# The state scan of a Mamba layer: eight of sixteen states go through TensorE, and GpSimd multiplies two

## The chip, the cores and the metric

One NeuronCore of one Trainium2 chip runs the whole program. The metric is the device time of one execution in microseconds (us). Kernels are told from each other by the median of several executions; a difference within 0.5% is taken as no difference.

The engines are TensorE (PE, with its weight loads shown apart as PEld), VectorE (DVE), ScalarE (ACT), GpSimd (POOL) and SyncE (SP, which only starts DMAs here). Each runs its own list of instructions in order, and they meet at semaphores.

## What is computed

The model is a chain of four blocks over x of 4 sequences x 1024 tokens x 256 channels: attention with a linear bias, two layers of windowed attention with a feed-forward part, a selective state scan (Mamba), and a mixture of 32 experts. The change touches only the core of the third:

```python
A = -jnp.exp(A_log)
def step(h, inputs):
    dt_t, x_t, B_t, C_t = inputs
    h = jnp.exp(dt_t[..., None] * A) * h + (dt_t * x_t)[..., None] * B_t[:, None, :]
    y = jnp.einsum('bds,bs->bd', h, C_t)
    return (h, y)
...
y = jnp.swapaxes(ys, 0, 1) + x * D
y = y * silu(z)
```

There are 512 inner channels d and 16 states s. For each sequence, channel and state a recurrence of first order runs over 1024 tokens; its result is multiplied by C (one row of 1024 values per sequence and state, the same for all channels) and summed over the 16 states.

## The kernel before

The program is nine phases one after the other. The scan is `phase_scan` (L2201), whose tiles have names beginning with H in the profile. It runs between the phase that makes its inputs and the mixture of experts.

**Tiling.** A tile is 128 channels of one sequence over all 1024 tokens: 4 sequences x 4 tiles = 16 tiles g. In each tile 16 states s are done one after the other, so there are 256 units n = (g, s). The text names a unit by its state within its tile: unit 2 is the third of a tile, and unit 16 is the first of the next.

**What every unit does.** ACT makes `decay` = exp(ndt x rate) in one of two PSUM buffers (L2367). POOL makes `feed` = ndu x B in one of four buffers (L2396, AHEAD = 4). DVE runs the recurrence (L2449).

**The product with C has three forms**, chosen by the letter of the state in `CLASS` (L2207):

- D: DVE itself multiplies by a row of C that was broadcast to 128 partitions (`times_c`, L2425), into `part`.
- P: the scan writes `handed`, and POOL multiplies (`shared_product`, L2406), into `pool_part`.
- T: the scan writes `turning`; PE transposes its eight 128x128 blocks (`turn`, L2490) into the PSUM tile `p_T`; ACT copies them back to SBUF, each scaled per partition by C (`weigh`, L2352), into `sT`; PE multiplies them with the negative identity, which turns them back and adds them (`bring`, L2500).

In the forms D and P, PE adds the part with four matmuls of the profile (`add`, L2508). All sums gather in one PSUM tile `p_y`, which starts with the term x * D (`skip_term`, L2469). DVE ends a tile with `tail` (L2433), which reads `p_y`; it is issued after unit 1 of the next tile.

**Orders that are written by hand.** They decide what waits behind what:

- ACT, for each n: decay(n), which waits until unit n-2 has been scanned (and, if it is D, multiplied); then weigh(n-2) if that unit is T.
- POOL, for each n: feed(n), which waits until unit n-4 has been scanned; then the product of unit n-2 if that is P.
- DVE, for each n: scan(n), times_c(n) if D, and after unit 1 the tail of the tile before.
- PE, for each n: add of the P unit n-4, bring of the T unit n-2, add of the D unit n-1, turn(n) if T. `skip_term` of a tile stands ahead of its first bring or add, and waits for the tail of the tile before, because `p_y` is single.
- SP loads the rows of B for each sequence, and rows of C broadcast for the states that are D or P (`weighted`).

Of the kernel before, what the change touches and what calls it, by code (L numbers as in the profile page):

```python
# [15 lines left out]
P = 128  # L16
# [2184 lines left out]
def phase_scan(nc, T):  # L2201
    with ExitStack() as ctx:
# [1 line left out]
        tiles = [(i, m) for i in range(SEQS) for m in range(XT)]  # L2204
        units = [(g, s) for g in range(len(tiles)) for s in range(NS)]
        NU = len(units)
        CLASS = "TTDPTDTDPTDTPDTD"  # L2207
        NB = SEQ // P
        HB = NB // 2
        NEXT_C = CLASS.index("P", NS // 2)  # L2210
        kind = [CLASS[s] for g, s in units]
        before = {c: list(accumulate((k == c for k in kind), initial=0)) for c in "TDP"}
        per = {c: CLASS.count(c) for c in "TDP"}
        weighted = [s for s in range(NS) if CLASS[s] != "T"]
        row_bytes = [16 if CLASS[s] == "T" else 32 for s in range(NS)]
        AHEAD = 4
# [18 lines left out]
        pool_part = a.sb("pool_part", [P, 2, SEQ])  # L2235
# [14 lines left out]
        p_summed = a.sem("p_summed")  # L2250
# [8 lines left out]
        def reached(eng, sem, value):  # L2259
            if value > 0:  # L2260
                eng.wait_ge(sem, value)

        def use_of(n):

            i = units[n][0] // XT
            return before["T"][n] + 1 + i + (n % (XT * NS) > (XT - 1) * NS + NEXT_C and i + 1 < SEQS)

        def use_of_c(i):
            return before["T"][(XT * i - 1) * NS + NEXT_C] + i if i else 0
# [111 lines left out]
        @block.gpsimd  # L2381
        def _(pool):
            pool.wait_ge(fixed, 48)
            for m in range(XT):
                nc.gpsimd.tensor_scalar(skip_diag[:, m, :], ident[:, :], skip[:, m:m + 1], None, ALU.mult)
            nc.gpsimd.tensor_scalar(minus[:, :], ident[:, :], -1.0, None, ALU.mult).then_inc(diag_ready, 1)

            def feeds(n):
                g, s = units[n]
                i, m = tiles[g]  # L2390
                if s == 0:
                    pool.wait_ge(dt_loaded[g % 2], 32 * (g // 2 + 1))
                if m == 0:
                    pool.wait_ge(row_loaded[s], row_bytes[s] * (i + 1))
                reached(pool, scanned, n - AHEAD + 1)
                nc.gpsimd.tensor_tensor(feed[:, n % AHEAD, :], ndu[:, g % 2, :], bs[:, s, :], ALU.mult  # L2396
                                        ).then_inc(fed, 1)

            def shared_product(n):
                g, s = units[n]  # L2400
                k = before["P"][n]
                if tiles[g][1] == 0:
                    pool.wait_ge(row_loaded[s], 32 * (tiles[g][0] + 1))
                pool.wait_ge(scanned, n + 1)
                reached(pool, p_summed, k - 1)
                nc.gpsimd.tensor_tensor(pool_part[:, k % 2, :], handed[:, k % 2, :], cs[:, weighted.index(s), :], ALU.mult  # L2406
                                        ).then_inc(pool_parted, 1)

            for n in range(NU + 2):
                if n < NU:  # L2410
                    feeds(n)
                if n >= 2 and kind[n - 2] == "P":
                    shared_product(n - 2)

        @block.vector
        def _(dve):
# [40 lines left out]
        @block.tensor  # L2457
        def _(pe):
            started = set()

            def skip_term(g):

                if g in started:
                    return
                started.add(g)
                reached(pe, yg_ready, g)
                pe.wait_ge(tail_loaded[g % 2], 32 * (g // 2 + 1))
                for c in range(2):
                    nc.tensor.matmul(p_y[:, c, :], skip_diag[:, tiles[g][1], :],  # L2469
                                     xs[:, g % 2, c * CHUNK:(c + 1) * CHUNK], start=True, stop=False)  # L2470

            def turn_c(i):
                u = use_of_c(i)
                pe.wait_ge(c_loaded, 16 * (i + 1))
                for h in range(2):
                    if u:
                        pe.wait_ge(copied, 2 * u + h - 1)
                    for b in range(HB):
                        at = (h * HB + b) * P
                        last = nc.tensor.transpose(p_T[:, h, b, 0:NS], c_rows[:, at:at + P], ident[0:NS, 0:NS])  # L2480
                    last.then_inc(turned, 1)

            def turn(n):
                u, k = use_of(n), before["T"][n]
                pe.wait_ge(scanned, n + 1)
                for h in range(2):
                    pe.wait_ge(copied, 2 * u + h - 1)
                    for b in range(HB):
                        at = (h * HB + b) * P
                        last = nc.tensor.transpose(p_T[:, h, b, :], turning[:, k % 3, at:at + P], ident[:, :])  # L2490
                    last.then_inc(turned, 1)

            def bring(n):
                g, s = units[n]
                skip_term(g)
                k = before["T"][n]
                for h in range(2):
                    pe.wait_ge(copied, 2 * use_of(n) + h + 1)
                    for b in range(HB):
                        last = nc.tensor.matmul(p_y[:, h, b * P:(b + 1) * P], sT[:, k % 2, h * HB + b, :], minus[:, :],  # L2500
                                                start=False, stop=False)
                last.then_inc(t_summed, 1)

            def add(n, src, done):
                g, s = units[n]
                skip_term(g)
                for c in range(2):
                    last = nc.tensor.matmul(p_y[:, c, :], minus[:, :], src[:, c * CHUNK:(c + 1) * CHUNK],  # L2508
                                            start=False, stop=s == NS - 1)
                last.then_inc(done, 1)  # L2510

            pe.wait_ge(fixed, 48)
            pe.wait_ge(diag_ready, 1)
            turn_c(0)
            for n in range(NU + 5):
                if 0 <= n - 4 < NU and kind[n - 4] == "P":
                    k = before["P"][n - 4]
                    pe.wait_ge(pool_parted, k + 1)
                    add(n - 4, pool_part[:, k % 2, :], p_summed)
                if 0 <= n - 2 < NU and kind[n - 2] == "T":  # L2520
                    bring(n - 2)
                if 0 <= n - 1 < NU and kind[n - 1] == "D":
                    k = before["D"][n - 1]
                    pe.wait_ge(parted, k + 1)
                    add(n - 1, part[:, k % 3, :], d_summed)
                if n < NU:
                    i = units[n][0] // XT + 1
                    if units[n] == (XT * i - 1, NEXT_C) and i < SEQS:
                        turn_c(i)
                    if kind[n] == "T":  # L2530
                        turn(n)
# [517 lines left out]
def build(nc, T):  # L3049
    with nc.allow_non_contiguous_dma(reason="weights' columns, biases and slots, a few elements each"):  # L3050
        phase_qkv(nc, T)
        phase_attention(nc, T)
        for layer in range(2):
            phase_window(nc, T, layer)
            phase_feed_forward(nc, T, layer, layer == 1)
        phase_front(nc, T)
        phase_scan(nc, T)
        phase_moe(nc, T)
# [21 lines left out]
```

## Time and profile before

| | us |
|---|---|
| median of 3 executions | 3718.92 (3718.04 to 3734.68) |
| the profiled execution | 3717.85 |
| its span in the profile | 3716.1 |
| around the span | 1.75 |
| the scan phase, from its first ACT decay to the end of its last tail | 2670.8 to 3405.4 |
| mean granted TensorE clock | 0.949 |

| engine, whole program | busy us | share |
|---|---|---|
| PE | 3243.4 | 87% |
| DVE | 2436.9 | 66% |
| ACT | 1875.8 | 50% |
| POOL | 1444.3 | 39% |

The phases follow each other without overlap, so these shares say little about a change in one of them. The scan takes about a fifth of the time and has its own limits; the stretch between two tails is one tile. In the timeline, pieces are named by tile, line and count, a number in brackets is the idle time of that engine before the piece, and the name behind it is what ended that idle time. Where PE's pieces overlap by some tenths of a us, that is the pipelining of matmuls: the distance from one start to the next is what counts.

### The profile page before, as it was taken

What the parts mean: (1) busy time and instruction counts of PE and PEld (TensorE: products, weight loads), DVE (VectorE), ACT (ScalarE), POOL (GpSimd) and SP (SyncE); (2) the same over time, 40 slices, a digit from 0 to 9 for tenths busy, and PEclk for the clock granted to TensorE, in tenths of its full rate; (3) what the DMA queues carried; (4) which work ended last, traced back from release to release, by engine and by line L of the source; (5) the groups of instructions that cost most, each with busy time, mean ns of one, the idle gap of its engine ahead of it and who ended that gap; (6) DMA issues with size and microseconds to landing.
All of it is one profiled execution on the core that took longest, in us unless ns stands there. A gap on an engine that the chain in (4) does not pass through costs nothing. (4 is left out here: it accounts for less than half of the span.)

```text
span 3716.1 us, 52305 instructions
## 1 busy us (share of the span) xinstructions
PE 3243.4 (87%) x18096; PEld 1976.8 (53%) x18096; DVE 2436.9 (66%) x4589; ACT 1875.8 (50%) x4007; POOL 1444.3 (39%) x993
## 2 busy tenths in 40 slices
PE   8599999879999799799999799799288888887898
PEld 4244444346666555466666455333156565555766
DVE  8488888456666522266666332389499999996633
ACT  2177777646666411166666311165377777774100
POOL 4101111122222211122222111134599999996523
PEclk9699999989999899899999899899599999999899
DMA  5956565120000141200000321233535151512874
GB/s 169 150 65 95 84 84 79 33 68 22 22 22 22 52 164 54 67 19 22 22 22 20 90 72 48 77 132 144 193 133 199 57 199 57 199 57 80 297 220 124
DMA packets 275715, 347.29 MB, mean 93 GB/s; under 512 B 70976, under 2 KB 206640, under 8 KB 274812
## 3 DMA queue, kind: packets, MB, share of 16 engines
q1 hardware_dynamic: 259596, 305.70, 30.1%
q10 hardware_dynamic: 10736, 25.94, 2.0%
q0 software_dynamic: 5120, 12.30, 0.9%
q8 instruction: 145, 2.38, 0.3%
q14 instruction: 118, 0.97, 0.1%
HBM read 227.72 MB, written 112.80 MB: 92 GB/s over the span
## 5 line engine op out<-in xcount | busy, mean ns | idle before, releaser
L2396 POOL TENSOR_TENSOR H_feed<-H_ndu,H_bs 128x1024 f32<-128x1024 f32 x256 | 595.2, 2364 | 5.8 <-DMA H_cs<-between_bc 3.1
L852 ACT ACTIVATE B_probs<-B_p_exp,B_key_bias 128x512 f32<-128x512 f32 (+3 forms) x768 | 394.8, 583 | 144.0 <-PE B_p_exp L910 113.4
L750 DVE TENSOR_REDUCE B_part_max<-B_p_max 128x1 f32<-128x512 f32 (+3 forms) x768 | 374.6, 545 | 84.0 <-PE B_p_max L874 81.5
L1283 ACT ACTIVATE D_probs<-D_scores,D_neg,D_rq 128x256 f32<-128x256 f32 x512 | 283.1, 573 | 289.1 <-DVE D_neg L1198 289.1
L2367 ACT ACTIVATE H_decay<-H_ndt,H_rate 128x1024 f32<-128x1024 f32 x256 | 287.8, 1125 | 196.3 <-DVE H_turning L2449 103.1
L1137 POOL TENSOR_TENSOR D_rnorm<-D_norm,D_power 128x8 f32<-128x8 f32 x64 | 106.2, 1659 | 506.6 <-DVE D_norm L1153 506.6
L871 PE MATMUL B_p_max<-B_k,B_q 100*128 100x512 bf16 (+3 forms) x768 | 256.9, 341 | 43.2 <-DMA B_key_bias<-in_key_bias 33.2
L1700 PE MATMUL E_p_ag<-E_hT,E_w 128*128 128x512 f32 x640 | 283.2, 602 | 2.1 <-ACT E_hT L1656 2.1
L2449 DVE TENSOR_TENSOR_SCAN H_turning<-H_decay,H_feed 128x1024 f32<-128x1024 f32 x112 | 253.5, 2274 | 23.2 <-POOL H_feed L2396 22.2
L2500 PEld LDWEIGHTS H_p_y<-H_minus,H_sT 128*128 128x128 f32 x1792 | 224.9, 200 | 76.2 <-ACT H_sT L2352 56.2
L2500 PE MATMUL H_p_y<-H_minus,H_sT 128*128 128x128 f32 x1792 | 233.4, 287 | 35.6 <-ACT H_sT L2352 35.6
L907 PE MATMUL B_p_exp<-B_q,B_k 100*128 100x512 bf16 (+3 forms) x768 | 250.3, 330 | 11.4 <-ACT B_probs L852 6.5
L1672 ACT ACTIVATE E_gated<-E_p_ag,E_b 128x512 f32<-128x512 f32 x96 | 62.6, 652 | 373.9 <-PE E_p_ag L1700 354.7
L2352 ACT ACTIVATE H_sT<-H_p_T,H_cT 128x128 f32<-128x128 f32 x896 | 242.9, 388 | 12.7 <-PE H_p_T L2490 12.3
L1345 PE MATMUL D_p_qk<-D_wqkv,D_hT 128*128 128x512 f32 x512 | 242.0, 616 | 1.1 <-ACT D_hT L1258 1.1
L1195 DVE CUSTOM_DVE_ANT_0 D_scores<-D_scores,D_mask 128x256 f32<-128x256 f32 x512 | 202.1, 457 | 55.6 <-PE D_scores L1372 55.3
L2449 DVE TENSOR_TENSOR_SCAN H_decay<-H_decay,H_feed 128x1024 f32<-128x1024 f32 x96 | 218.9, 2280 | 15.7 <-POOL H_feed L2396 15.5
L1700 PEld LDWEIGHTS E_p_ag<-E_hT,E_w 128*128 128x128 f32 x640 | 122.0, 193 | 155.5 <-issue 154.5
L1141 POOL TENSOR_TENSOR D_rnorm<-D_norm,D_power 128x8 f32<-128x8 f32 x64 | 129.9, 2029 | 188.3 <-DVE D_norm L1153 188.3
L1627 DVE SCALAR_TENSOR_TENSOR E_act_out<-E_p_ag,E_b,E_gated 128x512 f32<-128x512 f32 x96 | 67.7, 706 | 197.3 <-ACT E_gated L1672 197.3
L871 PEld LDWEIGHTS B_p_max<-B_k,B_q 100*128 100x128 bf16 x768 | 75.2, 98 | 221.4 <-DVE B_part_max L750 132.0
L2508 PE MATMUL H_p_y<-H_part,H_minus 128*128 128x512 f32 x384 | 185.0, 604 | 8.4 <-DVE H_part L2425 8.4
(259 smaller groups left out, 6874.9 us busy)
## 6 DMA issues: line engine op xcount, KB each, us to landing
H_bs<-between_bc SPq DMA_DIRECT2D x64, 512.0 KB, 7.5
H_cs<-between_bc SPq DMA_DIRECT2D x36, 512.0 KB, 8.2
B_q<-between_q_parts SPq DMA_DIRECT2D x96, 128.0 KB
B_k<-between_k_parts SPq DMA_DIRECT2D x96, 128.0 KB
between_slots_x<-E_clear ACTq DMA_DIRECT2D x4, 2570.0 KB, 22.0
I_xe<-between_slots_x ACTq DMA_DIRECT2D x32, 257.0 KB, 4.0
D_base<-between_z SPq DMA_DIRECT2D x64, 128.0 KB, 2.2
between_z<-D_z SPq DMA_DIRECT2D x64, 128.0 KB, 1.7
```

Source lines behind the costliest of these rows:

```text
L750: nc.vector.reduce_max(part_max[:, g % 2, kc, qb, h:h + 1], p_max[:, use % 3, 0:keys], AX.X).then_inc(maxed, 1)
L852: nc.scalar.activation(probs[:, x % PROBS, skip:512], p_exp[:, n % SCORES, skip:512], ACT.Exp, bias=key_bias[:, g % SETS, kb - 4 * Q + 4, ...
L871: last = nc.tensor.matmul(p_max[:, use % 3, 0:keys], q[0:KR, u, h, qb * P:(qb + 1) * P], k[0:KR, u, h, 512 * kc:512 * kc + keys], start=Tr ...
L907: last = nc.tensor.matmul(p_exp[:, n % SCORES, skip:512], k[0:KR, u, h, kb * P:(kb + 1) * P], q[0:KR, u, h, 512 * Q + skip:512 * Q + 512], ...
L1283: last = nc.scalar.activation(probs[:, place[m], :, :].rearrange("p a b -> p (a b)"), scores[:, place[m], :, :].rearrange("p a b -> p (a b ...
L1345: last = nc.tensor.matmul(p_qk[:, m, :], hT[:, i % 2, k, :], wqkv[:, k, m * INNER:(m + 1) * INNER], start=k == 0, stop=k == KD - 1)
L1700: last = nc.tensor.matmul(p_ag[:, m % 2, n, :], w1[:, k, at:at + P], hT[:, i % 2, k, :], **flags)
L2352: last = nc.scalar.activation(sT[:, k % 2, h * HB + b, :], p_T[:, h, b, :], ACT.Copy, scale=cT[:, i % 2, h * HB + b, s:s + 1])
L2367: nc.scalar.activation(decay[:, n % 2, :], ndt[:, g % 2, :], ACT.Exp, scale=rate[:, m, s:s + 1]).then_inc(decayed, 1)
L2396: nc.gpsimd.tensor_tensor(feed[:, n % AHEAD, :], ndu[:, g % 2, :], bs[:, s, :], ALU.mult).then_inc(fed, 1)
L2449: nc.vector.tensor_tensor_scan(out, decay[:, n % 2, :], feed[:, n % AHEAD, :], 0.0, ALU.mult, ALU.add).then_inc(scanned, 1)
L2500: last = nc.tensor.matmul(p_y[:, h, b * P:(b + 1) * P], sT[:, k % 2, h * HB + b, :], minus[:, :], start=False, stop=False)
```

## The change

`CLASS` becomes a strict alternation. There are now eight T (0, 2, 4, ... 14), six D (1, 3, 7, 9, 13, 15) and two P (5 and 11), where there were seven T, six D and three P (3, 8, 12). POOL makes the product of unit n-4 behind feed(n), and no more that of unit n-2. PE adds a P unit five iterations later, and no more four. The names that are worked out from `CLASS` follow: `weighted` has eight states for nine, so eight rows of C are broadcast, and `NEXT_C`, the state at which C of the next sequence is turned, is 11 for 8.

```diff
-        CLASS = "TTDPTDTDPTDTPDTD"
+        CLASS = "TDTDTPTDTDTPTDTD"
...
-            for n in range(NU + 2):
+            for n in range(NU + AHEAD):
                 if n < NU:
                     feeds(n)
-                if n >= 2 and kind[n - 2] == "P":
-                    shared_product(n - 2)
+                if n >= AHEAD and kind[n - AHEAD] == "P":
+                    shared_product(n - AHEAD)
...
-            for n in range(NU + 5):
-                if 0 <= n - 4 < NU and kind[n - 4] == "P":
-                    k = before["P"][n - 4]
+            for n in range(NU + 6):
+                if 0 <= n - 5 < NU and kind[n - 5] == "P":
+                    k = before["P"][n - 5]
                     pe.wait_ge(pool_parted, k + 1)
-                    add(n - 4, pool_part[:, k % 2, :], p_summed)
+                    add(n - 5, pool_part[:, k % 2, :], p_summed)
```

## Rows read from the trace of the kernel before

**Rows 1.** Busy time of each engine in one tile, by stretch; clock 1.00 is full

```profile
core 0: us, PE busy (x) PEld busy (x) DVE busy (x) ACT busy (x) POOL busy (x), PEclk, DMA share, GB/s
2911.00:2956.00 45.00, 38.21 (x209) 25.77 (x208) 43.47 (x24) 32.18 (x73) 43.82 (x20) 1.00 0.16 59
```

**Rows 2.** Groups of the scan phase: busy us, mean ns, idle before and releasers

```profile
L2396 POOL TENSOR_TENSOR H_feed<-H_ndu,H_bs 128x1024 f32<-128x1024 f32 x256 | 595.2, 2364 | 5.8 <-DMA H_cs<-between_bc 3.1 <-DMA H_bs<-between_bc 2.7
...
L2406 POOL TENSOR_TENSOR H_pool_part<-H_handed,H_cs 128x1024 f32<-128x1024 f32 x48 | 113.1, 2357 | 17.3 <-DVE H_handed L2449 17.3
```

**Rows 3.** Waits of the scan phase: total us, times, longest us

```profile
DVE H_decay L2449 <- POOL H_feed L2396: 15.5, 16, 2.6
ACT H_sT L2352 <- PE H_p_T L2490: 12.3, 8, 2.5
```

**Rows 4.** Timeline, DVE, from one tail to the next: start, us, piece

```profile
2909.30 1.20 DVE L2433 TENSOR_TENSOR H_sz<-H_p_y,H_sz 128x1024 f32<-128x1024 f32 x1
2910.42 2.29 DVE L2449 TENSOR_TENSOR_SCAN H_decay<-H_decay,H_feed 128x1024 f32<-128x1024 f32 x1
2912.81 1.23 DVE L2425 TENSOR_TENSOR H_part<-H_decay,H_cs 128x1024 f32<-128x1024 f32 x1
2913.95 2.28 DVE L2449 TENSOR_TENSOR_SCAN H_handed<-H_decay,H_feed 128x1024 f32<-128x1024 f32 x1
2916.15 2.27 DVE L2449 TENSOR_TENSOR_SCAN H_turning<-H_decay,H_feed 128x1024 f32<-128x1024 f32 x1
...
2946.54 2.30 DVE L2449 TENSOR_TENSOR_SCAN H_decay<-H_decay,H_feed 128x1024 f32<-128x1024 f32 x1 [0.91 <-POOL H_feed L2396]
...
2954.47 1.20 DVE L2433 TENSOR_TENSOR H_sz<-H_p_y,H_sz 128x1024 f32<-128x1024 f32 x1
```

**Rows 5.** Timeline, PE and ACT in the same tile

```profile
2911.00 1.88 PE L2469 MATMUL H_p_y<-H_xs,H_skip_diag 128*128 128x512 f32 x4
...
2918.45 1.12 ACT L2367 ACTIVATE H_decay<-H_ndt,H_rate 128x1024 f32<-128x1024 f32 x1 [1.07 <-DVE H_turning L2449]
2918.47 1.09 PE L2490 MATMUL H_p_T<-H_ident,H_turning 128*128 128x128 f32 x8 [0.30 <-DVE H_turning L2449]
2919.50 2.16 ACT L2352 ACTIVATE H_sT<-H_p_T,H_cT 128x128 f32<-128x128 f32 x8
2920.68 2.19 PE L2500 MATMUL H_p_y<-H_minus,H_sT 128*128 128x128 f32 x16 [1.12 <-ACT H_sT L2352]
2922.71 1.88 PE L2508 MATMUL H_p_y<-H_part,H_minus 128*128 128x512 f32 x4
2924.43 1.04 PE L2490 MATMUL H_p_T<-H_ident,H_turning 128*128 128x128 f32 x8
2925.30 1.88 PE L2508 MATMUL H_p_y<-H_pool_part,H_minus 128*128 128x512 f32 x4
2927.02 1.95 PE L2500 MATMUL H_p_y<-H_minus,H_sT 128*128 128x128 f32 x16
2928.80 1.88 PE L2508 MATMUL H_p_y<-H_part,H_minus 128*128 128x512 f32 x4
```

**Rows 6.** Timeline of the first tile, where DVE waits for ACT

```profile
2714.26 1.04 PE L2490 MATMUL H_p_T<-H_ident,H_turning 128*128 128x128 f32 x8
2714.98 2.18 ACT L2352 ACTIVATE H_sT<-H_p_T,H_cT 128x128 f32<-128x128 f32 x8 [2.52 <-PE H_p_T L2490]
2716.99 2.21 ACT L2367 ACTIVATE H_decay<-H_ndt,H_rate 128x1024 f32<-128x1024 f32 x2
2718.20 2.29 DVE L2449 TENSOR_TENSOR_SCAN H_turning<-H_decay,H_feed 128x1024 f32<-128x1024 f32 x1 [0.89 <-ACT H_decay L2367]
```

**Rows 7.** Timeline, PE, where a bring runs at a lower clock

```profile
2796.47 1.09 PE L2490 MATMUL H_p_T<-H_ident,H_turning 128*128 128x128 f32 x8 [1.39 <-DVE H_turning L2449]
...
2798.68 3.41 PE L2500 MATMUL H_p_y<-H_minus,H_sT 128*128 128x128 f32 x16 [1.12 <-ACT H_sT L2352]
```

**Rows 8.** Timeline, DVE, unit 7 of the first tile

```profile
2697.46 2.30 DVE L2449 TENSOR_TENSOR_SCAN H_decay<-H_decay,H_feed 128x1024 f32<-128x1024 f32 x1
```

## The prediction

> **What bounds the kernel now.** The phases run one after the other, so I read only the scan. The busy time of one tile comes first: in 45.0 us DVE works 43.47 and POOL 43.82, PE 38.21, ACT 32.18 [rows 1]. Two engines are nearly full, and the other two have room. The waits then say which of the two ends last: a D scan waits for a feed 16 times, 15.5 us in all [rows 3], and the timeline puts this once into every tile, ahead of unit 15 (0.91 us) [rows 4]. From tail to tail a tile takes 45.17 us (2909.30 to 2954.47) [rows 4]. So POOL is the bound, but only just. How far below it lies DVE? A D unit takes 3.53 us from scan to next scan (2910.42 to 2913.95), any other 2.19 (2913.95 to 2916.15 shows 2.20, later ones 2.18), the tail 1.12 [rows 4]. With 3.52 for D: 6 x 3.52 + 10 x 2.19 + 1.12 = 44.14 us. That is DVE's floor, and the change leaves it alone: still six D and ten others. **The whole prize is 1.03 us a tile, 15 us in all, 0.4%.**
>
> **Part 1, POOL.** It issues 18 operations a tile for 19, each 2.31 us from start to start (43.82 busy of 45.0, so 44.0 in 45.17, by 19 [rows 1]; 2.36 each in [rows 2], as they overlap a little): 41.7 us for 44.0. Its wait for `handed` (17.3 us in all [rows 2]) goes too: feed(n) and the product of unit n-4 wait for the same scan. POOL is then over 2 us a tile quicker than DVE and keeps up to four feeds in hand; the wait ahead of unit 15 goes: 0.9 us a tile. Nothing waits for the later product: PE wants it five iterations on, some 13 us after the scan, and it comes 5 us after. On SP the loads of the next sequence's rows 5 and 11 wait for it, and all rows queued behind them, some 2.5 us longer; they are needed 12 units later. Nothing. One broadcast row of 25 a sequence goes, from a queue that ends no wait after the start: nothing.
>
> **Part 2, PE and ACT, by their sums.** One add (1.72 us from start to start, 2922.71 to 2924.43) becomes a turn (0.87) and a bring (1.78 to 2.03) [rows 5]. PE: +1.1 us on 38.2. ACT: a weigh more, +2.0 to 2.2 on 32.2. Both stay below 44. By sums alone the change gains.
>
> **Part 3, the order around the tail.** Here I leave the sums and follow the queues, with these steps, all between starts [rows 5, 6]: turn to weigh 0.72 (2714.26 to 2714.98); weigh to its bring 1.18 where PE waits for it; weigh to the next decay 2.01; decay to weigh 1.06; decay to its scan 1.21 (2716.99 to 2718.20); bring to next 2.03 behind a running weigh, else 1.78; add or skip_term 1.72; turn to next 0.87.
>
> Time 0 is a tail's start. Before, units 0 and 1 are both T. Turn(1) is out of the way by the end of the tail, skip_term starts at 1.70 (2911.00), and the next turn is that of unit 4, at 9.17 (2918.47) [rows 4, 5]: between lie units 2 and 3, and that time just holds skip_term, two brings and an add (7.5 us).
>
> After, unit 1 is D and unit 2 is T. PE's order is skip_term, bring(0), add(1), turn(2), and skip_term waits for the tail. It starts at about 1.29 (tail 1.20, then a signal), bring(0) 3.01, add(1) 4.79, turn(2) **6.51**. Unit 2 starts its scan at 1.12 and is ready to be turned at 3.45. Turn(2) is 3.06 us late. On ACT, weigh(2) follows at 7.23, and behind it in the same queue stands decay(5): 9.24. So scan 5 starts at 10.45. DVE could have started it at 9.02 (1.12 + 2.19 + 3.52 + 2.19). **Stall 1.43 us.**
>
> It goes on: bring(2) 8.41, add(3) 10.44, turn(4) 12.16, weigh(4) 12.88, decay(7) 14.89, scan 7 16.10, which DVE could have begun at 14.83 (10.45 + 2 x 2.19). **Stall 1.27 us.** Then bring(4) 14.06, and as unit 5 is P there is no add: turn(6) 16.09, weigh(6) 17.03, bring(6) 18.21, add(7) 20.24, turn(8) 21.96; scan 8 has just ended. PE has caught up. Around the second P (turn(10) behind the added P, at 28.06; weigh 28.78; decay(13) 30.79; scan 13 32.00 for 31.90) another 0.10. Unit 17 starts at 43.42 and the next tail at 46.94.
>
> A tile so takes 44.14 + 1.43 + 1.27 + 0.10 = **46.94 us for 45.17: +1.77**. The same reckoning of the order of before gives 44.14 and POOL's wait, as measured, and that this chain exists is in the trace: in the first tile a turn was late (ACT idle 2.52 us), its weigh held up decay, and DVE stood still for 0.89 us [rows 6].
>
> **Part 4, ends.** Fourteen whole intervals between tails: 24.8 us. Last tile, from its tail on: its unit 15 would start 37.71 us after that tail for 37.24 before (2946.54 less 2909.30): +0.45. First tile: feed arrivals are the same in number of rows; POOL's product no longer stands between feeds, about 2 us better; the late turns of a cold PE cost 1.7 and 1.2 as above; I come to unit 7 at 2698.4 for 2697.46 [rows 8], and as unit 1 is now D the first tail comes another 1.3 later. No row shows this start, so bounds: from -1 to +4; I take +2.0. Sum so far 27.3 us.
>
> **Part 5, TensorE's clock.** In six tiles of 16 a bring behind a quiet stretch (idle 1.39, a turn, idle 1.12: 3.6 us from one product to the next) ran partly at 1.2 GHz, 3.41 us for 2.19 [rows 5, 7]; the add behind it was slow too, and PE about 1.5 us late. ACT waited for turns 8 times, 12.3 us: once 2.52 [rows 6], once at the very end, and six times about 1.3 behind such a bring; DVE never noticed these six, as there was slack [rows 3]. The order after has a new quiet stretch: from the end of add(15) at 44.4 to skip_term at 48.2, 3.9 us with only a turn in it. Behind it stand exactly skip_term, bring(0), add(1), turn(2), where every us is a stall of DVE. If it happens as often as before: 6 x 1.5 = 9 us. Its bounds are none and all 15: 0 to 22.5. Sum **36.3 us**. Against the profiled execution's 3717.85 that is 3754.1; the median lies 1.1 higher, so 3755.
>
> The Trainium skill, TensorE: Matmul & The Clock Gate, section HAM oscillation, says that idle stretches between bursts of matmuls send the clock back to half each time round a loop; its section on PE-mode transpose adds that a transpose does not keep it up. By that the fall would come behind every tail, which is the rival of 3768 below. The trace agrees with it in six of 16 tiles only.
>
> **Rivals.**
> - **The prize is won** (faster side): PE's lateness behind the tail does not reach decay, DVE runs at its floor. 15 x -1.03 = -15.5: 3703. For it: the sums of part 2, and that DVE has three `turning` and three `part` buffers. Against it: ACT's order puts decay(5) behind weigh(2) with no other way round [rows 6]. It decides if turn(2) comes 1.43 us earlier than 6.51, at 5.08.
> - **Half of it**: the first stall comes, but PE makes up the rest before unit 7 (bring(2) starts sooner behind weigh(2), or adds overlap more). 44.14 + 1.43 = 45.57: +0.40 x 15 = 6 us, with the start's +1: 3726.
> - **Half clock behind every tail**: 27.3 + 22.5 = 49.8: 3768. For it: the quiet stretch of 3.9 us in each tile. Against: stretches of 3.6 us did it in six tiles of 16.
> - **The change does not do what it says**: POOL still ends last, because the products bunch. 18 operations are 41.7 us; I give it almost nothing. A PE that stays behind for the whole tile (49 us a tile) would be 3780.
>
> **How the numbers follow.** Forecast 3755, by itself 3742 to 3764 (no low clock with a good start, to ten falls): 0.56. Half clock behind every tail, 0.15. Half of it, 0.13. The prize, 0.13. PE behind all through, 0.03. The measurement of this kernel tells about 0.5% from no change, 18.6 us, which is more than the whole prize: faster by more has 0.03, slower (over 3737.5) the first, second and last, 0.74, and within it the rest, 0.23. The range leaves out the prize and the far tail: 3719 to 3777.
>
> **What would show it.** Right: tail to tail near 47 us; DVE waits for decay ahead of units 5 and 7 of each tile, about 1.4 and 1.3 us, and no more for feeds; POOL's idle time is 5 us a tile; turn(2) starts 6.5 us after the tail's start; some skip_terms and brings behind the tail at half clock. Wrong: tails 44.2 us apart with no wait of DVE, or its waits at other units; turn(2) before bring(0); a wait for `pool_part`.

## The result and the profile after

| | before | after |
|---|---|---|
| median | 3723.2 us | 3774.01 us (3768.62 to 3778.5, 4 executions) |
| ratio | 1 | 1.0139, 95% interval 1.0115 to 1.0163 |
| profiled execution | 3717.85 us | 3770.14 us |
| mean granted clock | 0.949 | 0.946 |

The change costs 1.4%, about 51 us. The forecast was 3755 with a range of 3719 to 3777.

The profiled executions are 52.3 us apart. In the one of after, the first scan starts 4.4 us later, at 2680.13 for 2675.70. The phases ahead of it are untouched, and in the kernels below, which do not touch them either, it starts anywhere between 2670.2 and 2697.7. So what is measured inside the scan is more reliable than the difference of two whole executions. From the first scan to the end of the last tail the scan phase grew by 46.9 us, and the phase behind it by 1.0. Of the first kernel below with turn(2) ahead, two of five executions were disturbed, at 8665.77 and 10821.92 us, and its median and ratio are those of the other three.

First the waits of the scan phase of after (the view of rows 3: total us, times, longest us).

```profile
ACT H_sT L2352 <- PE H_p_T L2490: 93.6, 42, 5.7
...
PE H_p_y L2469 <- DVE H_sz L2433: 44.2, 15, 3.2
DVE H_handed L2449 <- ACT H_decay L2367: 39.0, 15, 4.4
...
DVE H_decay L2449 <- ACT H_decay L2367: 19.0, 17, 1.2
```

Before, DVE waited for a feed once in each tile [rows 3]. Now POOL waits for DVE, and DVE waits for ACT's `decay`: 15 times ahead of a P unit, 39.0 us, and 17 times ahead of a D unit, 19.0 us. ACT in turn waits for PE's transposes, 93.6 us for 12.3 [rows 3], and PE's `skip_term` (L2469) waits for the tail 15 times. That is the chain of the prediction, from its end to its start.

The timeline of one tile shows the steps. It answers to rows 4 and 5; start, us, piece, and in brackets the idle time before it.

```profile
2778.73 1.22 DVE L2433 TENSOR_TENSOR H_sz<-H_p_y,H_sz 128x1024 f32<-128x1024 f32 x1
...
2779.86 2.28 DVE L2449 TENSOR_TENSOR_SCAN H_turning<-H_decay,H_feed 128x1024 f32<-128x1024 f32 x1
...
2780.00 1.98 PE L2469 MATMUL H_p_y<-H_xs,H_skip_diag 128*128 128x512 f32 x4 [3.17 <-DVE H_sz L2433]
...
2781.82 1.95 PE L2500 MATMUL H_p_y<-H_minus,H_sT 128*128 128x128 f32 x16
...
2783.60 1.88 PE L2508 MATMUL H_p_y<-H_part,H_minus 128*128 128x512 f32 x4
...
2785.32 1.04 PE L2490 MATMUL H_p_T<-H_ident,H_turning 128*128 128x128 f32 x8
...
2786.04 2.18 ACT L2352 ACTIVATE H_sT<-H_p_T,H_cT 128x128 f32<-128x128 f32 x8 [2.75 <-PE H_p_T L2490]
...
2788.06 2.21 ACT L2367 ACTIVATE H_decay<-H_ndt,H_rate 128x1024 f32<-128x1024 f32 x2
...
2789.26 2.29 DVE L2449 TENSOR_TENSOR_SCAN H_handed<-H_decay,H_feed 128x1024 f32<-128x1024 f32 x1 [1.40 <-ACT H_decay L2367]
...
2794.92 2.30 DVE L2449 TENSOR_TENSOR_SCAN H_decay<-H_decay,H_feed 128x1024 f32<-128x1024 f32 x1 [1.19 <-ACT H_decay L2367]
```

Set the tail's start, 2778.73, to zero: skip_term 1.27, bring(0) 3.09, add(1) 4.87, turn(2) 6.59, weigh(2) 7.31, decay(5) 9.33, scan 5 10.53. The prediction had 1.29, 3.01, 4.79, 6.51, 7.23, 9.24 and 10.45. The waits are 1.40 and 1.19 us for 1.43 and 1.27. The next tail starts at 2825.87, so the tile takes 47.14 us, for 45.17 before [rows 4] and 46.94 forecast.

Not every tile is like that. In nine of the fifteen tiles that begin with a tail, the wait ahead of unit 5 is 2.81 to 4.38 us. Here is the same place in such a tile, and under it the busy time of PE and PEld, DVE, ACT and POOL, the granted clock, DMA share and GB/s in stretches behind the tail (the first two of this tile, the last of the tile above).

```profile
2921.66 1.22 DVE L2433 TENSOR_TENSOR H_sz<-H_p_y,H_sz 128x1024 f32<-128x1024 f32 x1
...
2922.93 3.78 PE L2469 MATMUL H_p_y<-H_xs,H_skip_diag 128*128 128x512 f32 x4 [3.20 <-DVE H_sz L2433]
...
2926.51 3.13 PE L2500 MATMUL H_p_y<-H_minus,H_sT 128*128 128x128 f32 x16
...
2935.13 2.29 DVE L2449 TENSOR_TENSOR_SCAN H_handed<-H_decay,H_feed 128x1024 f32<-128x1024 f32 x1 [4.34 <-ACT H_decay L2367]
```

```profile
2922.00:2926.00 4.00, 3.07 (x4) 1.52 (x5) 4.00 (x3) 1.79 (x2) 2.11 (x2) 0.52 0.32 131
2926.00:2930.00 4.00, 4.00 (x19) 3.25 (x18) 3.90 (x3) 0.23 (x1) 3.82 (x2) 0.63 0.77 260
...
2779.00:2783.00 4.00, 3.00 (x15) 2.05 (x16) 4.00 (x3) 1.79 (x2) 2.08 (x2) 1.00 0.32 131
```

The granted clock is 0.52 and 0.63 there, so mostly 1.2 GHz, and skip_term takes 3.78 us for 1.98. The text calls this a fall of the clock. The DMA share is 0.32 in the first of these stretches, where the clock had fallen, and 0.32 in the one where it had not, so the loads do not tell the two apart. The excess of the nine waits over 1.40 adds up to 18.0 us, 2.0 each.

Of the six tiles without a fall, three are the first of a sequence, and they are not like the others: PE stood idle ahead of their skip_term for 2.23, 1.70 and 2.22 us only, where it did for 3.13 to 3.20 us in the other twelve. So nine of twelve like places had a fall; why the other three had none stays open. The reason for the shorter stretch is in the tile ahead, the last of a sequence. There PE transposes the C rows of the next sequence (`turn_c`, L2480, at unit 11), waits for ACT's copies on the way, and is late up to the end of the tile. Here is that in one tile, and the skip_term behind it:

```profile
2857.50 0.39 PE L2480 MATMUL H_p_T<-H_ident,H_c_rows 16*128 16x16 f32 x4 [0.97 <-ACT H_sT L2352]
2858.44 0.41 PE L2480 MATMUL H_p_T<-H_ident,H_c_rows 16*128 16x16 f32 x4 [0.56 <-ACT H_sT L2352]
...
2875.70 1.98 PE L2469 MATMUL H_p_y<-H_xs,H_skip_diag 128*128 128x512 f32 x4 [2.23 <-DVE H_sz L2433]
```

POOL's part came out as forecast: it did less work and had time.

```profile
L2396 POOL TENSOR_TENSOR H_feed<-H_ndu,H_bs 128x1024 f32<-128x1024 f32 x256 | 596.9, 2363 | 101.1 <-DVE H_turning L2449 57.6 <-DVE H_handed L2449 37.7 <-DMA H_bs<-between_bc 4.2
...
L2406 POOL TENSOR_TENSOR H_pool_part<-H_handed,H_cs 128x1024 f32<-128x1024 f32 x32 | 75.5, 2360 | 0.0
```

Its feeds now have 101.1 us of idle time ahead of them for 5.8, and its products none for 17.3 [rows 2].

### The profile page after: what moved, and what is told of

The parts are those of the page before. It is cut to its first block and busy times, and to the rows that moved or that the text cites. A ratio compares the mean times of both kernels' runs of the same rounds, so it can differ in the third digit from the quotient of the medians.

```text
span 3768.3 us, 53069 instructions
## 1 busy us (share of the span) xinstructions
PE 3269.1 (87%) x18416; PEld 2016.7 (54%) x18416; DVE 2438.1 (65%) x4589; ACT 1908.7 (51%) x4135; POOL 1409.3 (37%) x977
## 5 line engine op out<-in xcount | busy, mean ns | idle before, releaser
L2396 POOL TENSOR_TENSOR H_feed<-H_ndu,H_bs 128x1024 f32<-128x1024 f32 x256 | 596.9, 2363 | 101.1 <-DVE H_turning L2449 57.6
L2500 PE MATMUL H_p_y<-H_minus,H_sT 128*128 128x128 f32 x2048 | 273.7, 286 | 74.1 <-ACT H_sT L2352 74.1
L2352 ACT ACTIVATE H_sT<-H_p_T,H_cT 128x128 f32<-128x128 f32 x1024 | 278.6, 388 | 95.3 <-PE H_p_T L2490 93.6
L2500 PEld LDWEIGHTS H_p_y<-H_minus,H_sT 128*128 128x128 f32 x2048 | 254.3, 195 | 124.7 <-ACT H_sT L2352 100.4
L2449 DVE TENSOR_TENSOR_SCAN H_turning<-H_decay,H_feed 128x1024 f32<-128x1024 f32 x128 | 291.4, 2276 | 21.9 <-POOL H_feed L2396 21.9
```

The costliest lines, as they stand in the source:

```text
L2352: last = nc.scalar.activation(sT[:, k % 2, h * HB + b, :], p_T[:, h, b, :], ACT.Copy, scale=cT[:, i % 2, h * HB + b, s:s + 1])
L2449: nc.vector.tensor_tensor_scan(out, decay[:, n % 2, :], feed[:, n % AHEAD, :], 0.0, ALU.mult, ALU.add).then_inc(scanned, 1)
```

## The experiments

All were compared with the kernel before on the same chip, whose median in those comparisons was 3720.9 to 3726.9 us.

**Which part of the change costs: the class or the distance.** The new CLASS, with the product two units behind and PE's add four:

```diff
 (kernel before)
-        CLASS = "TTDPTDTDPTDTPDTD"
+        CLASS = "TDTDTPTDTDTPTDTD"
```

> Only the new CLASS; POOL's product follows its unit by two and PE adds it four iterations on, as in the kernel before. Theory: POOL has 5 us of room in a tile, so its waits for handed come back and cost nothing; the same stalls ahead of units 5 and 7, 3768 to 3780 us. Rival (the later product is what costs, by the order of PE's add behind the second P, or of the feeds): near the kernel before, 3720 to 3740.

Measured: 3770.78 us, ratio 1.0117 (1.0095 to 1.0139). The letters alone make the whole loss. Its waits in the scan phase (the profiled execution is the slowest of its five, with a fall in 11 of 15 tiles, which is why the second line is above the 39.0 of the kernel after):

```profile
POOL H_pool_part L2406 <- DVE H_handed L2449: 103.5, 30, 7.6
DVE H_handed L2449 <- ACT H_decay L2367: 43.9, 15, 4.4
```

POOL waits 103.5 us for `handed`, in the place of the feeds' idle time, and DVE never waits for POOL in a whole tile. With this CLASS the distance gains nothing that the medians show: the intervals of the two ratios overlap.

**The distance alone.** The new distance cannot be given to the old CLASS as it is: unit 12 would be added behind unit 15, which closes the sum. So the product went to three units behind, and PE's list stayed.

```diff
 (kernel before)
-            for n in range(NU + 2):
+            for n in range(NU + 3):
...
-                if n >= 2 and kind[n - 2] == "P":
-                    shared_product(n - 2)
+                if n >= 3 and kind[n - 3] == "P":
+                    shared_product(n - 3)
```

> The kernel before with its own CLASS; only POOL's product follows its unit by three for two. Theory (POOL was the bound by its work and by its waits for handed, 17.3 us in all): most of these waits go, POOL needs 44.0 us a tile and DVE 44.1, so tails 44.2 to 44.4 us apart and 12 to 15 us less than the kernel before: 3706 to 3712. Rival (POOL's waits only took up room it had): tails stay at 45.2, within 3 us of the kernel before.

Measured: 3708.22 us, ratio 0.9955 (0.9933 to 0.9978). By its interval this is faster than both kernels, but 0.45% is less than the 0.5% that the medians are trusted with here, so the trace has to carry it. The group of its product (as in rows 2), and two tails:

```profile
L2406 POOL TENSOR_TENSOR H_pool_part<-H_handed,H_cs 128x1024 f32<-128x1024 f32 x48 | 113.5, 2364 | 1.1 <-DVE H_handed L2449 0.8
```

```profile
2904.24 1.20 DVE L2433 TENSOR_TENSOR H_sz<-H_p_y,H_sz 128x1024 f32<-128x1024 f32 x1
...
2948.38 1.20 DVE L2433 TENSOR_TENSOR H_sz<-H_p_y,H_sz 128x1024 f32<-128x1024 f32 x1
```

44.14 us from tail to tail, which is the floor that the prediction worked out for DVE. Nine of the fourteen intervals are 44.14 or 44.15, the others 44.21 to 44.32, and together they are 13.9 us shorter than before. The product's idle time fell from 17.3 [rows 2] to 1.1 us. The prize of the change was real, and a later product alone, with the old letters, was enough to win it.

**The eighth T, or the D at unit 1.** Two kernels take the two apart. The first has the changed kernel's counts, eight T, six D and two P, with units 1 and 2 changed about:

```diff
 (kernel after)
-        CLASS = "TDTDTPTDTDTPTDTD"
+        CLASS = "TTDDTPTDTDTPTDTD"
```

> The changed kernel with units 1 and 2 changed about, CLASS TTDDTPTDTDTPTDTD: the same eight T, six D, two P, the same work on each engine. Theory: behind the tail skip_term, two brings and two adds now have until 10.5 us for turn(4), and that suffices; tails 44.2 to 44.5 us apart, 3705 to 3716 us, little low clock as the quiet stretch ahead of skip_term is short again. Rival (number of T): 3765 to 3775, unchanged.

Measured: 3718.18 us, ratio 0.9978 (0.9965 to 0.999). Nine of the fourteen intervals between its tails inside the phase are 44.51 or 44.52 us, the others 45.2 to 45.8; the longest wait of DVE inside a tile after the first is 1.0 us. The expected range ended 2 us lower, but the loss of 51 us is gone with the work of every engine unchanged. The second kernel has the counts of before, seven T, and a D at unit 1:

```diff
 (kernel before)
-        CLASS = "TTDPTDTDPTDTPDTD"
+        CLASS = "TDTPTDTDPTDTPDTD"
```

> The kernel before with units 1 and 2 of each tile changed about, CLASS TDTPTDTDPTDTPDTD: seven T, six D, three P, distances as before. Theory (D at unit 1 brings turn(2) behind skip_term, bring(0) and add(1)): turn(2) starts 6.5 us after the tail, decay(5) at 9.2, scan 5 at 10.45, and as unit 3 is P here DVE would have been there at 7.7: wait of 2.8 us ahead of unit 5, none ahead of unit 7; tails 46.9 us apart and 48 to 50 where the clock falls, 3745 to 3770. Rival (the eighth T is the cause): tails stay at 45.2, 3718 to 3730.

Measured: 3781.06 us, ratio 1.0174 (1.0154 to 1.0194). DVE waits ahead of unit 5 in every tile, 2.75 us where the clock held (2.76 by the prediction's steps), 4.2 to 5.7 us where it fell, as here:

```profile
2779.09 1.21 DVE L2433 TENSOR_TENSOR H_sz<-H_p_y,H_sz 128x1024 f32<-128x1024 f32 x1
...
2780.36 3.51 PE L2469 MATMUL H_p_y<-H_xs,H_skip_diag 128*128 128x512 f32 x4 [3.56 <-DVE H_sz L2433]
...
2787.20 1.04 PE L2490 MATMUL H_p_T<-H_ident,H_turning 128*128 128x128 f32 x8
...
2791.13 2.30 DVE L2449 TENSOR_TENSOR_SCAN H_decay<-H_decay,H_feed 128x1024 f32<-128x1024 f32 x1 [4.27 <-ACT H_decay L2367]
```

So a D at unit 1 costs the time with seven T as with eight, and eight T without it cost none. It measured above its expected 3745 to 3770. The clock fell in 11 of 15 tiles, 23.7 us in all, and a tile without a fall took 47.7 to 47.8 us for the 46.9 expected: 0.5 of it is a wait for a feed ahead of unit 15, as the third P unit is back.

**Is it PE's order, and is turn(2) all of it?** PE's turn(2) ahead of bring(0) and add(1), behind skip_term:

```diff
 (kernel after, PE)
+                first = n < NU and kind[n] == "T" and units[n][1] == 2
+                if first:
+                    if units[n][1] == 2:
+                        skip_term(units[n][0])
+                    turn(n)
...
-                    if kind[n] == "T":
+                    if kind[n] == "T" and not first:
                         turn(n)
```

> The changed kernel, with PE's list altered in one place of each tile: skip_term, then turn(2), then bring(0) and add(1); nothing else moves. Theory (PE's order behind the tail: turn(2) stands behind bring(0) and add(1), ACT carries that on to decay(5)): turn(2) starts about 3.5 us after the tail's start, scan 5 at 9.0, no waits of DVE for decay ahead of units 5 and 7; tails about 44.3 us apart, so 14 x 4.1 less than the changed kernel, 3710 to 3716 us, and a fall of TensorE's clock behind the tail costs nothing (turn(2) at 4.8 is still in time). Rival (the eighth T as such overloads PE and ACT, the order is a detail): the waits move to other units, tails stay at 47 us or more, 3765 to 3775.

Measured: 3762.85 us, ratio 1.0103 (1.0074 to 1.0132). The theory was wrong, and the rival's 3765 to 3775 is nearly met. I had forgotten what the edit does not remove. Between skip_term and turn(4) still lie bring(0), add(1), bring(2) and add(3). Worked again, and run again for its timeline:

> The same kernel as the one with turn(2) alone ahead, since its profiled execution was disturbed. Theory, worked again after its times (3753 to 3767): only the first stall goes; bring(0), add(1), bring(2) and add(3) still lie between skip_term and turn(4), which starts 11.3 us after the tail for 9.2, so decay(7) comes at 14.0 and scan 7 at 15.3 for 13.4: no wait ahead of unit 5, 1.9 us ahead of unit 7, tails 46.1 us apart, more where the clock falls; 3745 to 3765. Rival (number of T): waits at other units too, and further on in the tile.

Measured: 3764.26 us, ratio 1.0101 (1.0072 to 1.0129). Of its waits for decay, none is ahead of unit 5, and those ahead of unit 7 are 1.82 to 1.85 us in four tiles where the clock held and 2.85 to 4.11 in the others. Here is one of the latter:

```profile
2798.97 1.22 DVE L2433 TENSOR_TENSOR H_sz<-H_p_y,H_sz 128x1024 f32<-128x1024 f32 x1
...
2803.74 1.04 PE L2490 MATMUL H_p_T<-H_ident,H_turning 128*128 128x128 f32 x8
...
2811.62 1.04 PE L2490 MATMUL H_p_T<-H_ident,H_turning 128*128 128x128 f32 x8
...
2815.56 2.30 DVE L2449 TENSOR_TENSOR_SCAN H_decay<-H_decay,H_feed 128x1024 f32<-128x1024 f32 x1 [3.10 <-ACT H_decay L2367]
```

Turn(2) starts 4.77 us after the tail even in this tile with a fall, for 6.59 without one in the kernel after, and turn(4) only at 12.65. The intervals between tails are 46.3 to 48.8 us. So the signs that were named for the rival did come: the wait moved to another unit and most tiles stayed above 47 us. Its cause, the number of T, is ruled out by the two kernels above and not by this one. What this one shows is that the order of two instructions only moves the backlog. PE stands idle up to the tail (3.17 us) and then has more to do than fits.

**ACT's order.** Weigh(2) behind decay(5):

```diff
 (kernel after, ACT)
-                    if kind[n - 2] == "T":
+                    if kind[n - 2] == "T" and units[n - 2][1] != 2:
                         weigh(n - 2)
+                    if units[n - 2][1] == 3:
+                        weigh(n - 3)
```

> The changed kernel; ACT does decay(5) ahead of weigh(2) and not behind it, in every tile. Theory (ACT only carries on what PE's order makes late): the wait ahead of unit 5 goes to nothing, weigh(2) starts 8.0 us after the tail for 7.2, turn(4) comes later, and the wait ahead of unit 7 grows from 1.2 to 3.5 us; tails about 47.8 us apart where the clock holds, but low clock behind the tail is partly hidden: 3770 to 3786 us. Rival (ACT's order is the cause): both waits shrink, tails about 45.5, 3725 to 3735.

Measured: 3780.22 us, ratio 1.0157 (1.0102 to 1.0212). Ten of fourteen tiles take 47.82 to 47.95 us, with no wait ahead of unit 5 and 3.37 us ahead of unit 7, for 3.5 expected. ACT's order places the loss and does not make it.

**All turns ahead.** The condition is `units[n][1] > 0`, with skip_term ahead only at unit 2.

> The changed kernel; in every iteration but that of unit 0 PE's turn(n) comes ahead of the added P, bring(n-2) and add(n-1); behind the tail skip_term stays first. Theory: the stalls behind the tail go as in the kernel with turn(2) alone moved, and the 0.1 to 0.2 us ahead of unit 13 too: tails at DVE's floor, 44.2 us; 3705 to 3712 us, 0 to 4 us less than that kernel. Rival (brings and adds now come late and hold up the tail, which waits for all sums): DVE waits for p_y ahead of the tail, 1 to 3 us in each tile, 3720 to 3750.

Measured: 3738.33 us, ratio 1.0036 (1.0012 to 1.006), inside the rival's range: tiles of 45.4 to 46.8 us. The rival's wait is there, but smaller than the 1 to 3 us that it named: 0.35 to 0.6 us ahead of eleven of the first fifteen tails. In most tiles DVE also waits some 0.26 us for decay ahead of units 3 and 15:

```profile
2966.47 1.23 DVE L2433 TENSOR_TENSOR H_sz<-H_p_y,H_sz 128x1024 f32<-128x1024 f32 x1 [0.36 <-PE H_p_y L2508]
...
2970.15 2.30 DVE L2449 TENSOR_TENSOR_SCAN H_decay<-H_decay,H_feed 128x1024 f32<-128x1024 f32 x1 [0.26 <-ACT H_decay L2367]
```

This order wins 36 us over the changed kernel, but the sums are done later, and the tail, which needs them all, waits. The same with nine T, five D, two P (`CLASS = "TTDTPTDTTDTPTDTD"`):

> PE's order as in the kernel with all turns ahead, and CLASS TTDTPTDTTDTPTDTD: nine T, five D, two P. Theory: DVE's floor falls by the 1.33 us of one product to 42.9 us a tile, PE about 38, ACT about 36, POOL 41.7: if the order holds, tails 42.9 to 43.3 us apart, 3683 to 3692 us, below both kernels. Rival (a ninth T is too much for PE and ACT): waits for decay behind the two neighbouring T, tails above 45, 3720 or more.

Measured: 3777.8 us, ratio 1.0118 (1.0066 to 1.017). Here the tail waits 2.07 to 3.71 us for p_y in each tile, and a P unit mostly 0.5 to 3.4 us for decay. The lower floor of DVE was no use.

**The clock.** PE gets work in the quiet stretch ahead of skip_term: 16 matmuls that nobody reads, into the half of `p_T` that ACT has done with.

```diff
 (kernel after, PE, skip_term)
                 started.add(g)
+                if g:
+                    pe.wait_ge(copied, 2 * use_of(NS * g) + 1)
+                    for b in range(16):
+                        nc.tensor.matmul(p_T[:, 0, b % HB, :], ident[:, :], minus[:, :], start=True, stop=True)
                 reached(pe, yg_ready, g)
```

> The changed kernel with 16 matmuls of 128 columns more ahead of each skip_term but the first; they write into the part of p_T that weigh(16) has done with, and nobody reads them: 1.9 us of work in PE's quiet stretch before the tail's end. Theory: the falls of the clock (9 of 15 tiles, DVE's wait ahead of unit 5 then 2.8 to 4.4 us for 1.4) go, all waits there are 1.4 us, tails 47.1 to 47.3 us apart: 18 to 20 us less than the changed kernel, 3750 to 3756. Rival (those tiles are late for another reason, a DMA or the row loads, or the clock falls all the same): 3770 to 3775; if the added work itself delays skip_term, more.

Measured: 3771.72 us, ratio 1.012 (1.0098 to 1.0143). The time hardly changed, but its parts did: the wait ahead of unit 5 was 2.64 to 2.72 us in 12 of 15 tiles and 3.58 to 3.63 in three, without the scatter of before. Each matmul shows as two records, so the added work took 3.84 us and not 1.9, and held skip_term up by 1.4 us (2.65 us after the tail's start for 1.27). The wait grew by 1.3. With 8 matmuls:

> The kernel with added matmuls in the quiet stretch, with half as many: 1.9 us of them, as the first version was meant to have; its 3.84 us kept the clock up but made skip_term 1.4 us late. Theory: no fall and no delay, DVE waits 1.4 us ahead of unit 5 in every tile, tails 47.1 to 47.3 us apart: 3748 to 3758. Rival (the work must go on up to skip_term, or the clock falls by a rhythm of its own): some waits of 2.8 to 4.4 us stay, 3760 to 3772.

Measured: 3752.83 us, ratio 1.0097 (1.0078 to 1.0116), 21 us below the changed kernel's 3774.01. Twelve waits ahead of unit 5 are 1.40 us, and ten of fourteen intervals are 47.12 to 47.15 us. The stretch in another tile:

```profile
2863.72 2.05 PE L2469 MATMUL H_p_T<-H_minus,H_ident 128*128 128x128 f32 x16 [0.93 <-ACT H_sT L2352]
2863.76 1.22 DVE L2433 TENSOR_TENSOR H_sz<-H_p_y,H_sz 128x1024 f32<-128x1024 f32 x1
...
2865.61 1.88 PE L2473 MATMUL H_p_y<-H_xs,H_skip_diag 128*128 128x512 f32 x4
```

skip_term takes 1.88 us. This is one of the other three tiles, the first of a sequence each, where the turn ahead of the added work is late by the `turn_c` of the tile before, so that the added work ended late and the wait was 1.80 to 2.33 us. No skip_term behind a tail is slow any more. The falls behind the tail are thus a matter of PE's quiet stretch, and worth 18 us in the profiled execution.

## Why the prediction was right

**The side and the mechanism** were right, and each step of part 3 up to the scan of unit 7 came within 0.1 us (16.19 us after the tail for 16.10). The two waits are 1.40 and 1.19 us in each tile without a fall; by part 2's sums alone the change would have won. The trace of before held what this part needed: the order of the lists in the code, the step times from one undisturbed tile, and one place where DVE had already waited for ACT for this reason [rows 6].

**Part 1** was right, and the three-unit distance shows that its prize of 1.03 us a tile was there.

**The size.** The sum had 36.3 us where the scan phase grew by 46.9. Two terms were mis-sized:

- Part 5, the clock. It had 6 falls at 1.5 us, 9 us; the trace has 9 at 2.0, 18.0 us. Behind the tail, skip_term and bring run slowly with no slack behind them, and a fall cost 1.4 to 3.0 us. The count of six was one short already for the kernel before, where the bring of the first tile, ahead of the rows 6, was slow as well (3.78 us). The bound of all 15 tiles was not met: six tiles had none, three of them behind the idle stretch that `turn_c` shortens, which the prediction did not see. That rival's time, 3768, is nevertheless nearer than the forecast, for the wrong reason: 9 x 2.0 is close to 15 x 1.5.
- Part 4, the first tile: +2.0 taken, -1.4 measured (51.46 us from first scan to first tail for 52.85). The bounds of -1 to +4 missed it. The two late turns that it counted on, 1.7 and 1.2 us, did not hold DVE up: its waits in this tile are 0.83, 0.37 and 0.79 us for feeds and 0.19 for decay, and unit 7 starts 20.31 us after the first scan, for 21.76 before and 22.7 expected.

The rest is small: 0.19 us more in a quiet tile (47.13 for 46.94), 2.7 us over 14; 0.99 us ahead of unit 15 of one tile, where a fall met the lateness from `turn_c`; and 0.8 us more wait of the last tail for PE. With these the sum comes to 46.4.

**The rivals.** "The prize is won" failed as its own text said it would: turn(2) did not come before 5.08, and when it did (at 4.77, in the kernel with turn(2) ahead) the wait ahead of unit 5 was gone, as that point says. What that text missed is turn(4): the loss then stood ahead of unit 7. "Half of it" has no tile in the trace: the second wait is 1.19 us in all fifteen.

## What to carry to other kernels

Busy sums of 34 and 39 us in a tile of 44 do not say that the work fits. Write down for each in-order list what stands behind the instruction that waits for another engine's last result, here PE's skip_term behind the tail, and give the work behind it the time until the next thing that the bound engine needs; two letters changed about in a table did 56 us here (3774.01 to 3718.18) with the same work. When a change has two parts, try each alone: a distance of three units, one number, won 0.45% without the part that lost 1.4%. And when one instruction is moved ahead, work out the one behind it too.

## What the runs showed of the hardware

- TensorE at 1.2 GHz came in nine of the 12 places of one execution of the kernel after where it had been idle for 3.13 to 3.20 us behind eight transposes, and in none of the three places where that was 1.70 to 2.23 us. With seven T and a D at unit 1 the idle time was 3.55 to 3.59 us, and it came in 11 of 15. Matmuls of 2.05 us put into the stretch ended it. It is not sure to come in any one tile, and where the next engine has no slack its price is 1.4 to 3.0 us, 2.0 on average, on three operations that take 5.3 us from the first start to the next turn at full clock.
- A matmul of 128x128 fp32 shows as two records and takes 0.24 us at full clock: 16 of them took 3.84 us.
- The start of the scan phase differed by 27 us between executions of kernels that are the same up to there (first scan at 2670.2 to 2697.7 us). Differences of less than that are read inside the phase.
